# A state-space layer and a gated MLP with adapters in fp32 on one core: the down projection as a 2x2 block product with seven products

## What is computed

```python
def lora_add(base, inp, A, B):                     # A, B chosen per batch row by lora_indices
    t = jnp.einsum('bri,bni->bnr', A[0][lora_indices], inp)
    return base + jnp.einsum('bor,bnr->bno', B[0][lora_indices], t) * 0.5
x = x + conv(x)                                    # x: (32, 64, 1024)
gate = lora_add(jnp.einsum('bnh,fh->bnf', x, W_gate), x, A_gate, B_gate)   # F = 2752
up   = lora_add(jnp.einsum('bnh,fh->bnf', x, W_up), x, A_up, B_up)
act  = jax.nn.silu(gate) * up
down = lora_add(jnp.einsum('bnf,hf->bnh', act, W_down), act, A_down, B_down)
return x + down
```

## Time and profile before

| | |
|---|---|
| median of 3 runs | 1744.29 us (1742.24 to 1745.56) |
| the profiled execution | 1744.96 us, span 1743.3 us, mean granted clock 0.979 |
| PE, DVE, ACT, POOL busy | 94%, 53%, 32%, 6% of the span |
| down projection (first matmul to last add) | from 1210.51 to 1740.7 us of the span |
| DMA | 278 MB, 160 GB/s over the span |

### The profile page before, as it was taken

How to read it: one execution, slowest core, us unless ns; L and a number is a source line. 1 busy time by engine, 2 the same in 40 slices (tenths; PEclk the granted TensorE clock), 3 DMA queues, 4 the chain that set the end, 5 groups by cost and what they waited for, 6 DMA issues and landing times.

```text
span 1743.3 us, 20961 instructions
## 1 busy us (share of the span) xinstructions
PE 1634.4 (94%) x8224; PEld 1399.2 (80%) x8224; DVE 921.3 (53%) x1182; ACT 565.8 (32%) x678; POOL 109.0 (6%) x169
## 2 busy tenths in 40 slices
PE   1988969999999999699999999998999999999999
PEld 1988857888888888578888888886888888888887
DVE  6444466665666655676655666566325325424422
ACT  2211234333333333353333333334224224324321
POOL 4300063410000000000000000000000000000000
PEclk9999979999999999799999999998999999999999
DMA  8998677743333333433333333326547547646652
GB/s 300 359 352 327 213 240 214 224 142 97 97 97 102 107 107 109 134 95 97 107 107 105 108 103 101 97 73 209 171 130 229 168 139 219 178 135 217 180 139 61
DMA packets 157637, 278.42 MB, mean 160 GB/s; under 512 B 56323, under 2 KB 73539, under 8 KB 156995
## 3 DMA queue, kind: packets, MB, share of 16 engines
q1 hardware_dynamic: 104034, 234.19, 42.1%
q0 software_dynamic: 13440, 25.86, 4.8%
q10 hardware_dynamic: 40064, 17.04, 3.5%
HBM read 237.26 MB, written 65.31 MB: 174 GB/s over the span
## 4 chain that ended last, share of the span: by engine, by line
PE 87%; DMA 6%; DVE 4%; issue 2%; ACT 1%; SPq 0%; DVEq 0%; ACTq 0%
PE ps L769 80%; PE ps L754 6%; DMA tt<-k_pad 2%; DMA k_pad<-ksb 1%; DMA x_keep<-xt 1%; DMA raw<-a_gu_sel 1%; DMA xraw<-x_keep 1%; ACT whi L963 1%; DVE xlo L1485 1%; DVE wlo L1485 1%; DMA draw<-act_keep 0%; DVE xraw L1485 0%; DMA raw<-wgu 0%; ACT b12hi L963 0%; DVE xres L1679 0%
## 5 line engine op out<-in xcount | busy, mean ns | idle before, releaser
L769 PE MATMUL ps<-xhi,whi 128*128 128x512 f32 (+1 forms) x1080 | 421.5, 390 | 27.0 <-ACT cc L963 10.9
L769 PE MATMUL ps<-xlo,whi 128*128 128x512 f32 (+1 forms) x1080 | 420.4, 389 | 0.0
L769 PE MATMUL ps<-xhi,wlo 128*128 128x512 f32 (+1 forms) x1080 | 419.1, 388 | 0.0
L963 ACT ACTIVATE whi<-raw 128x1024 fp32r<-128x1024 f32 (+3 forms) x202 | 198.0, 981 | 581.5 <-PE ps L769 545.2
L1485 DVE TENSOR_TENSOR wlo<-raw,whi 128x1024 fp32r<-128x1024 f32 (+1 forms) x190 | 219.2, 1155 | 307.2 <-ACT whi L963 306.9
L769 PE MATMUL ps<-dhi,whi 128*128 128x512 f32 (+2 forms) x760 | 288.0, 379 | 3.7 <-DVE xres L1679 3.7
L769 PE MATMUL ps<-dlo,whi 128*128 128x512 f32 (+2 forms) x760 | 286.6, 377 | 0.0
L769 PE MATMUL ps<-dhi,wlo 128*128 128x512 f32 (+2 forms) x760 | 286.4, 377 | 0.0
L769 PEld LDWEIGHTS ps<-xhi,whi 128*128 128x128 f32 x1080 | 207.3, 192 | 66.4 <-issue 11.2
L769 PEld LDWEIGHTS ps<-xhi,wlo 128*128 128x128 f32 x1080 | 206.6, 191 | 41.5
L769 PEld LDWEIGHTS ps<-xlo,whi 128*128 128x128 f32 x1080 | 207.3, 192 | 37.4
(11 more groups left out here) (167 smaller groups left out, 1670.4 us busy)
## 6 DMA issues: line engine op xcount, KB each, us to landing
raw<-wgu SPq DMA_DIRECT2D x84, 512.0 KB, 6.6
tt<-k_pad SPq DMA_DIRECT2D x64, 512.0 KB, 9.7
raw<-wd SPq DMA_DIRECT2D x64, 512.0 KB, 3.8
loraw<-bgu_sel SPq DMA_DIRECT2D x84, 256.0 KB, 4.4
act_keep<-up SPq DMA_DIRECT2D x42, 512.0 KB, 3.1
draw<-act_keep SPq DMA_DIRECT2D x84, 256.0 KB, 7.1
bgu_sel<-bgu POOLq DMA_DIRECT2D x32, 336.0 KB, 7.1
raw<-wd SPq DMA_DIRECT2D x32, 320.0 KB, 3.0
```

Source lines behind the costliest of these rows:

```text
L769: return nc.tensor.matmul(out, w, x, start=start, stop=stop, skip_group_check=True)
L963: return nc.scalar.activation(out, in_, ACT.Copy)
```

## The change

The down projection becomes a 2x2 block product with seven products as well. Tiles of F are paired (the host permutes them, `PERM`), rows are taken in units of 1,024, and there are 16 steps of seven products with five tiles each; a step covers one unit u, one half `ch` of the 20 tiles and one pair of column tiles. Tile 20 and the rest of F come in `tails` in eight of the steps, the adapter's A in `down_a` in steps 1, 4, 9 and 12. The result of the first half of F is stored in a new buffer `y_first` and added in the second half.

The sums that it needs are formed during gate/up: after every odd step DVE writes four sums of activations over `gq` and `vv` (`act_sums`), and SP stores them to `act_sums`; in every step but the last of a unit DVE forms four sums of 128 columns of W_down (`weight_sums`), which SP brings in (`sums_in`) and stores (`sums_out`). `up` gets a second buffer. Weight units now have 640 columns, a ring of 6, and are split 4 ahead; activations have 35 tiles that are exchanged in steps 3/4, 7/8 and 11/12.

```diff
+RING = 6
+AHEAD = 4
...
             def store(n):
                 sp.wait_ge(s_mul, n + 1)
...
+                if f % 2:
+                    blk = f // 2
+                    sp.wait_ge(s_tq, 4 * (10 * u + blk + 1))
+                    sp.dma_start(tq_d[u, blk, 0:3].rearrange("k p t -> p k t"),
+                                 gq[:, :].rearrange("p (k t) -> p k t", k=3)).then_inc(s_tst, 16)
+                    sp.dma_start(tq_d[u, blk, 3], vv[:, :]).then_inc(s_tst, 16)
...
@@ SP, order behind the last gate/up step
+            load_act(0, 0, 5)
+            sp.wait_ge(s_swst, 16 * 40)
+            load_act(0, 0, 6)
+            for k, p in enumerate(PRODUCTS):
+                sp.wait_ge(s_p, prod(N - 1, p))
+                for t in range(7 + 4 * k, 11 + 4 * k):
+                    load_act(0, 0, t)
+                for i in {"P2": (0,), "P7": (1, 2), "P4": (3,), "P3": (4, 5)}.get(p, ()):
+                    load_unit(i)
+            for i, key in enumerate(DOWN):
+                step = key[1]
+                if i + RING < len(DOWN):
+                    load_unit(i + RING)
...
+                    if step % 4 == 3 and step < DSTEPS - 1:
+                        u, ch = (step + 1) // 8, (step + 1) // 4 % 2
+                        q = PRODUCTS.index(key[2])
+                        sp.wait_ge(*act_free(u, ch, 5 * q))
+                        for t in range(5 * q, 5 * q + 5):
+                            load_act(u, ch, t)
@@ PE
+            def down_product(step, p):
+                slot = unit_ready(("m", step, p))
+                if step % 4 == 0:
+                    pe.wait_ge(s_alo, ATILE[u, ch, 5 * q + 4])
...
+                if p == "P6":
+                    pe.wait_ge(s_y1, step + 1)
+                if p == "P4":
+                    pe.wait_ge(s_yd, step + 1)
+                for k in range(5):
+                    last = passes(bank[p], cols(rhi[slot], k), cols(rlo[slot], k), ahi[5 * q + k][:, :], alo[5 * q + k][:, :],
+                                  k == 0 and p in ("P1", "P2", "P5", "P7"))
@@ ACT
             def v(n):
+                if n % FT and n % FT % 2 == 0:
+                    act.wait_ge(s_tst, sums_stored(n - 1))
...
             def gu_to_down():
                 for t in range(4):
-                    d_hi(0, t)
+                    act_hi(0, 0, t)
+                unit_hi(0)
                 c1(N - 1)
...
+            for i, key in enumerate(DOWN):
+                if key[0] == "m":
+                    if p == "P2" and step:
+                        y_store(step - 1)
+                    if p == "P5" and step:
+                        res_in(step)
+                    if p == "P7":
+                        y_c1(step)
+                    if p == "P4":
+                        y_v(step)
+                if i + AHEAD < len(DOWN):
+                    unit_hi(i + AHEAD)
+                if key[0] == "m":
+                    nxt, tiles = next_acts(step, p)
+                    for t in tiles:
+                        act_hi(nxt // 8, nxt // 4 % 2, t)
@@ DVE
             def d(n):
+                if n % FT and n % FT % 2 == 0:
+                    dve.wait_ge(s_tst, sums_stored(n - 1))
...
+            def act_sums(n):
+                dve.wait_ge(s_mul, n + 1)
+                dve.wait_ge(s_c12, n + 1)
+                sub(gq[:, 0:T], even[:, T:2 * T], even[:, 0:T]).then_inc(s_tq, 1)
+                sub(gq[:, T:2 * T], odd[:, T:2 * T], even[:, T:2 * T]).then_inc(s_tq, 1)
+                dve.wait_ge(s_tq, base + 1)
+                sub(gq[:, 2 * T:3 * T], odd[:, T:2 * T], gq[:, 0:T]).then_inc(s_tq, 1)
+                dve.wait_ge(s_tq, base + 3)
+                sub(vv[:, :], odd[:, 0:T], gq[:, 2 * T:3 * T]).then_inc(s_tq, 1)
...
             for n in range(N):
                 if n % FT:
                     mul(n - 1)
+                    if (n - 1) % FT % 2:
+                        act_sums(n - 1)
...
                     w_lo("u2", n + 1)
+                    weight_sums(n)
```

More of the change, by code:

```diff
@@ L114, in raw_slot @@
         return 2 * (i % FT % 2)
[L115 to L132, removed]
+    return 2 * (i % FT % 2) + 1
 def raw_loads():
@@ L181, with result, last_result, piece @@
+ATILE = order_of_acts()
+def result(s, op):
+    n = 0
+    for r in range(s + 1):
+        ops = ("sums", "v", "d", "b") + (("e", "f") if r % 8 >= 4 else ())
+        if r == s:
+            return n + ops.index(op) + 1
+        n += len(ops)
+def last_result(s):
+    return result(s, "f" if s % 8 >= 4 else "b")
+def piece(n):
+    return n if n < FT - 1 else n - 1
 CAB, CPH, CPOS, CMASK, CAL, CBE, CNAL = 0, 64, 128, 136, 140, 141, 142
@@ new lines, in down_a @@
+            def down_a(step, x, kh, g):
+                u, ch = step // 8, step // 4 % 2
+                slot = unit_ready(("td", step, x, kh, g))
+                quads = [PRODUCTS.index(p) for p in TD_QUADS[x, kh]]
+                first = ch == 0 and kh == 0 and g == 0
+                if step % 8 == 4:
+                    pe.wait_ge(s_alo, max(ATILE[u, ch, 5 * q + 4] for q in quads))
+                if first:
+                    if u:
+                        pe.wait_ge(s_tde, 6 * u)
+                    else:
+                        pe.wait_ge(s_c12, N - 1)
+                out = half(ps[4 + GRP[x]], g)
+                for k in range(5):
+                    for q in quads:
+                        for y in (ahi, alo):
+                            last = mm(out, cols(rhi[slot], k), half(y[5 * q + k], g), first, False)
+                            first = False
+                signal(last)
@@ new lines, in down_a_tail @@
+            def down_a_tail(step, x):
+                u, i = step // 8, GRP[x]
+                slot = unit_ready(("tdt", step, x))
+                pe.wait_ge(s_alo, ATILE[u, "tail", 3])
+                for g in range(2):
+                    for k, rows in enumerate((P, FR)):
+                        for y in (ehi, elo):
+                            last = mm(half(ps[4 + i], g), rhi[slot][0:rows, (2 * g + k) * P:(2 * g + k + 1) * P],
+                                      half(y[2 * i + k][0:rows], g), False, False)
+                signal(last)
```

832 lines of the change are left out of this document (466 added, 366 removed).

## The result

The changed kernel takes 1813.5 us (median of four runs, 1810.6 to 1817.3), the kernel before 1744.9: a ratio of 1.040, 95% interval 1.037 to 1.042. The forecast was 1763 with a range of 1722 to 1792. The direction was right, the size was not: 18.6 us more were forecast, and the profiled executions differ by 65.6 us (spans 1808.9 and 1743.3).

What follows compares the result with a forecast made beforehand. The prediction took TensorE's matmul spacing as the bound; -44.8 (matmuls), -7.1 (sweep gaps), +23 (even steps), +4.5 (halves), +12 (transition), +27 (exchanges) and +4 (end) gave +18.6, so 1763 us, range 1722 to 1792.

Steps and rivals of the forecast that it cites:

- The mechanism in the even steps: Gate/up, every second step: d waits for the activation sums' 1 MB store, PE stands 1.3 us; +23 us.
- the 17 us wait at the last P6: From gate/up to down: P6 waits 17 us for ACT's copy cc, 8.8 more; whole term +12.
- the step between the halves: Gate/up between the halves: the B11 reload is issued later, behind the sums of step 19; +4.5 us.
- the end of the span: After the last matmul: four adds, then four stores, instead of one each; +4 us.
- the sign: Whole kernel: slower than before, +18.6 us; chance of slower 0.69.
- the exchanges: Down steps 3/4, 7/8, 11/12: tile loads and splits come late for PE; +15 and twice +6, 27 us.
- A: Rival, whole kernel: everything new hides and PE stays the bound throughout; 1706 us, chance 0.13.
- B: Rival, gate/up: the sums' store lands within 3.3 us, d is not late, down as forecast; 1740 us, chance 0.20.
- C: Rival: the landing takes 6.0 us (+26) and PE starts at half clock after long waits; 1799 us, chance 0.17.
- C's second half: PE starts at half clock after each long wait; +10 us with five more such waits.
- Nothing on PE waits for this by itself: Gate/up, every step: the weight sums shift c12 and the chain behind it by 0.9 us without holding PE.
- the down projection: From the last P6 to the end of the span: 17.7 us shorter, with fewer matmuls (-44.8) and sweep gaps gone (-7.1).

Runs made afterwards that it cites:

- e1: Against the changed kernel: a step's four weight sums stand one step later on DVE, behind mul and the activation sums; 1779.7 us.
- e7: Against the changed kernel: later activation tiles neither loaded nor split, down steps reuse the first 35 tiles, part of the work left out; 1772.5 us.
- e8: Against the changed kernel: residual loads of down steps 1 to 15 left out; 1789.8 us.
- s2: Changed kernel with later weight sums, T1 and T3 stored by their own DMA, and residuals loaded from a copy in 2 KB rows; timed again, 1753.0 us.
- e9: Against the changed kernel: both the later activation tiles (as in e7) and the residual loads of steps 1 to 15 (as in e8) left out; 1774.0 us.

## Why the prediction was wrong

**Right.** The mechanism in the even steps, its size (a landing of 4.2 us, pairs of 43.2 us), the 17 us wait at the last P6, the step between the halves (+5.7 for +4.5), and the end of the span. That the sign was right rests on these and on the exchanges. Of the rivals, A is refuted. B's condition, a landing within 3.3 us, was not met (4.2), and neither was C's of 6.0. C's second half, PE at half clock after long waits, did happen, and in some cases after waits of 2.3 to 2.5 us too.

**The step that failed first**: "Nothing on PE waits for this by itself", of weight_sums. The prediction counted the four adds (0.9 us) and not their load, which stands last in SP's queue, and it did not ask how long that load takes while the gathers run: 12 us. Of the 17.7 us in the first seven steps, e1 removed 13.7. In the regular steps the prediction did count the 0.9 us, within d's 1.3 us of lateness: without them its own numbers leave 0.4, and e1 measured 0.3 a pair. There the term was right in kind and small in size, 19 forecast and 23.5 measured.

**The second**: the down projection. For the stretch from the last P6 to the end the sum had -17.7; it measured +13.5, 31 us more. This is the larger miss.
- The exchanges: +27 forecast, 37.4 measured (558.1 less e7's 520.7). The term took DMA issues at 0.4 us and the results out and in as 5.8 us of traffic. It missed that the residuals come in 256-byte pieces, which take 16.5 us to land beside the tiles and hold ACT for 12.7. Rows of 2 KB gave 11.6 us back, some 9 of them at the exchanges. Its split was wrong too: 13, 14 and 10 us where it had 6, 15 and 6, because the 14 us of adapter matmuls in steps 4 and 12 stand behind the waits, most of which come in steps 3 and 11.
- The rest, 20.8 us, stays without exchange (520.7 against 499.9) and is what PE's timeline of e7 shows over the matmul count. Step 0 takes 9.7 more where 3.2 were counted, which makes 6.5: PE waits 6.7 us for alo, and the granted clock is 0.71 in the 10 us behind that wait. Steps 4 and 12 take 8.7, of which 5.3 are the wait for the adapter's rows and 2.8 the slow matmuls of `down_a_tail`; the prediction had neither. The waits for cc in steps 2, 8 and 10 come to 5.4 with the matmuls behind them, where the prediction had "nothing". These make 20.6.

What stays open: the 17 us of the exchange that are there without residual loads (in e8 PE's waits at the exchanges are 12.8 us, 9.8 of them ended by DVE, whose adds and splits share one order; no run changes that order alone); and whether the 17 us at the last P6 are set by bandwidth, since only orders were tried.

## What to carry to other kernels

Work that is added "beside" a chain brings its transfers with it: ask of each new load when it is issued, what else fills the queue then, and what stands in order behind its consumer. Where two small delays end in one wait, each alone looks like the cause; price them by removing one at a time and then both. And when an edit takes a wait away and the time stays, look in the trace for where the wait went before calling the place harmless. A transfer's pieces matter once its queue has to share the engines, so look at bytes per packet before moving the issue elsewhere.

## What the runs showed of the hardware

Issuing four DMAs of 1,024 pieces of 256 bytes held ACT's queue for 12.7 us at the exchange and for 3.0 to 7.4 without it (e7), against 3.3 for the same bytes in rows at the exchange (s2). Sixteen matmuls of 256 columns that alternate between 128 and 64 rows start 0.21 us apart (e7), others of 256 columns 0.120. A wait of 0.87 us left the granted clock at 1.00. In the 4 us behind a wait of 2.50 us, with no pause on PE in the 21 us ahead of it, two stood at 0.50, the lower of the two levels; in e9 a wait of 2.41 us did the same; in e7 waits of 2.50 and 2.46 us in the same place left it at 1.00. So a wait of this length brings the half clock in some executions and not in others. The ten us behind the end of the 17 us wait and of the 6.7 us one had 0.82 and 0.71. The Trainium skill (TensorE: Matmul & The Clock Gate, "HAM oscillation") tells of such half-clock spells after waits for DMA between groups of matmuls; the trace agrees for the long waits, and here waits for ACT and DVE did it. In the windows of the first exchange the core moved 326 GB/s with pieces and 351 with rows.
